# One attention and expert block on one core: the residual's x formed on VectorE from the projections' x

## The reference, cut to what matters

```python
def _layernorm(x, eps=1e-05):
    m = mean(x); v = var(x)
    return (x - m) / sqrt(v + eps)

def attn(x, ln1_w, Wq, Wk, Wv, rel_bias, scale, Wo, ln2_w, W1, W2):
    xn = rms_norm(x, ln1_w)                     # eps 1e-6
    q, k, v = heads(xn @ Wq), heads(xn @ Wk), heads(xn @ Wv)    # 16 heads of 8
    q, k = normalize(q), normalize(k)
    attn = (q @ k.T + bias) * scale, causal, softmax
    y = (attn @ v) @ Wo + x                     # <- the residual's x
    z = relu(rms_norm(y, ln2_w) @ W1) @ W2
    return z + y

x = L0_attn_x                                   # 8 images of 512 tokens of 128, float32
x = x + _layernorm(attn(_layernorm(x), ...))
x = x + _layernorm(moe(_layernorm(x), ...))     # top 2 of 8 experts
```

## Time and profile before

| | us |
|---|---|
| median of 3 runs | 609.92 |
| lowest and highest | 609.04, 613.66 |
| the profiled execution | 612.49 |
| span in the profile (first to last instruction) | 610.7 |
| mean granted TensorE clock | 0.955 of full speed |
| DMA | 55.85 MB, mean 91 GB/s |

### The profile page before, as it was taken

How to read it: one execution, slowest core, us unless ns; L and a number is a source line. 1 busy time by engine, 2 the same in 40 slices (tenths; PEclk the granted TensorE clock), 3 DMA queues, 4 the chain that set the end, 5 groups by cost and what they waited for, 6 DMA issues and landing times.

```text
span 610.7 us, 13818 instructions
## 1 busy us (share of the span) xinstructions
PE 532.2 (87%) x4568; PEld 386.2 (63%) x4569; DVE 382.8 (63%) x1083; ACT 396.6 (65%) x873; POOL 329.4 (54%) x337
## 2 busy tenths in 40 slices
PE   6876899989889899799899897899778979999992
PEld 5552355656466456465556564798678879999940
DVE  6627465783994974999947767363766434555344
ACT  3357898879779788878897786355353434554415
POOL 4012535536618888438877357176437754454426
PEclk9757799999999999999999999599999999999997
DMA  8755331223214323213734612022112332222074
GB/s 199 111 140 115 110 99 57 78 76 103 67 41 126 102 68 115 77 36 123 178 109 148 145 51 49 11 60 64 37 44 66 89 89 62 59 62 61 18 275 137
DMA packets 48285, 55.85 MB, mean 91 GB/s; under 512 B 7868, under 2 KB 42559, under 8 KB 46064
## 3 DMA queue, kind: packets, MB, share of 16 engines
q1 hardware_dynamic: 43872, 46.59, 28.3%
q0 software_dynamic: 4352, 8.47, 4.2%
HBM read 37.19 MB, written 18.36 MB: 91 GB/s over the span
## 4 chain that ended last, share of the span: by engine, by line
PE 49%; DVE 23%; POOL 11%; ACT 7%; issue 7%; DMA 3%; DVEq 1%; ACTq 0%; POOLq 0%; SPq 0%
PE SC L806 13%; PE OA L816 6%; PE OA L683 5%; PE M L757 4%; PE M L721 4%; POOL slots L1591 3%; DVE SS L1218 2%; POOL RZ L1577 2%; PE SC L665 2%; DVE arena L406 2%; DVE A L1477 2%; ACT arena L927 2%; DVE STP L1287 1%; PE SC L669 1%; PE M L649 1%
## 5 line engine op out<-in xcount | busy, mean ns | idle before, releaser
L927 ACT ACTIVATE arena<-SC 128x1024 f32<-128x1024 f32 x160 | 163.0, 1033 | 20.8 <-PE SC L670 12.3
L806 PE MATMUL SC<-arena 128*128 128x128 f32 (+1 forms) x864 | 110.8, 279 | 10.9 <-DVE arena L1385 10.9
L1597 POOL DMA_INDIRECT ytok<-YSA,XGA x72 | 74.8, 1038 | 80.4 <-ACT YSA L1030 71.5
L806 PEld LDWEIGHTS SC<-arena 128*128 128x128 f32 (+1 forms) x864 | 102.5, 186 | 14.0 <-DVE arena L1385 12.8
L683 PE MATMUL OA<-arena 128*32 128x256 f32 (+1 forms) x1536 | 91.4, 357 | 10.0 <-DVE arena L1251 6.1
L1591 POOL DMA_INDIRECT slots<-XBA,IDX x64 | 74.4, 1162 | 47.6 <-DVE IDX L1336 31.1
L1024 ACT ACTIVATE arena<-SC 128x256 f32<-128x256 f32 (+1 forms) x144 | 39.2, 324 | 78.2 <-PE SC L806 78.1
L1379 DVE TENSOR_TENSOR arena<-arena,SC 128x256 f32<-128x256 f32 (+1 forms) x144 | 44.2, 348 | 70.0 <-ACT arena L1024 70.0
L683 PEld LDWEIGHTS OA<-arena 128*32 128x32 f32 x1536 | 39.4, 110 | 49.6 <-issue 19.8
L406 POOL TENSOR_TENSOR arena<-arena 128x512 f32<-128x512 f32 x32 | 41.5, 1298 | 53.8 <-ACT arena L927 53.4
L816 PE MATMUL OA<-arena 128*128 (+1 forms) x432 | 60.2, 275 | 0.7 <-DVE arena L1379 0.7
(11 more groups left out here) (216 smaller groups left out, 1002.1 us busy)
## 6 DMA issues: line engine op xcount, KB each, us to landing
arena<-parts SPq DMA_DIRECT2D x90, 192.0 KB
parts<-arena SPq DMA_DIRECT2D x16, 384.0 KB, 2.5
XGA<-slots SPq DMA_DIRECT2D x72, 65.0 KB
arena<-ytok SPq DMA_DIRECT2D x8, 512.0 KB, 6.9
X<-in_L_attn_x SPq DMA_DIRECT2D x4, 512.0 KB, 5.3
arena<-toe SPq DMA_DIRECT2D x16, 128.0 KB, 5.9
out<-X SPq DMA_DIRECT2D x8, 256.0 KB, 2.3
arena<-parts SPq DMA_DIRECT2D x12, 96.0 KB
```

The costliest lines, as they stand in the source:

```text
L806: mm = pe.matmul(SC[0:n, r % 2, 512 * m + P * c:512 * m + P * (c + 1)], WSEL[r % 2][:, I * m + i0:I * m + i0 + n], XGT[r % 2], start=True, ...
L927: act.activation(EB[u], SC[:, n % 2, :], ACT.Exp).then_inc(exp_done, 1)
L1597: pool.indirect_dma_start(out=ytok_d.ap(), out_offset=bass.IndirectOffsetOnAxis(ap=XG[r][:, D + 1:D + 2].bitcast(I32), axis=0), in_=YS[r], ...
```

## The change

- XA, the semaphore xa_rdy and the function `xa` with its four activations per image go.
- At wo, DVE forms the sum from the projections' x: Y = XAR x RAT + M1, with one factor RAT per token, in four scalar_tensor_tensor of 128x128 in place of one addition of 128x512.
- XAR must live until then. It becomes XARS, three buffers, taken in turn; ACT waits for the transposes and the wo of the image three before.
- RAT is made in `x_roots` by two more DVE instructions, ahead of the one that signals st_rdy: residual's root times projections' root times the projections' variance.
- To make room, the scratch SCM of `slot_table` goes; the table uses one scratch in NW in place, so that its two reductions no longer stand back to back.

```diff
-ACT_AT = (dict(..., xar=-7, xa=1),
-    dict(..., h3=11, xa=0))
+ACT_AT = (dict(..., xar=-7),
+    dict(..., h3=11))
...
-        XA = sb("XA", [P, T, D])
+        XARS = [sb(f"XAR{r}", [P, T, D]) for r in range(2)] + [arena[:, 29184:29696].rearrange("p (t c) -> p t c", t=T)]
-        XAR = arena[:, WALL0 + 6656:WALL0 + 7168].rearrange("p (t c) -> p t c", t=T)
-        NWA = sb("NWA", [P, P])
-        NWB = sb("NWB", [P, P])
-        NWC = sb("NWC", [P, P])
+        RAT = sb("RAT", [P, NT])
+        NW = sb("NW", [P, 3 * P])
+        NWA, NWB, NWC = (NW[:, P * k:P * (k + 1)] for k in range(3))
-        SCM = sb("SCM", [P, 2, max(FIRST, EARLY - FIRST, STILES - EARLY), E])
+        PAST = NW[:, P:3 * P]
...
-                turn4(M0, XAR).then_inc(m0_full, 1)
+                turn4(M0, XARS[b % 3]).then_inc(m0_full, 1)
...
-                if b > 0:
-                    act.wait_ge(m0_full, USES0 * (b - 1) + 1)
-                norm(XAR, b, 1).then_inc(xar_rdy, 1)
-
-            def xa(b):
-
-                if b > 0:
-                    act.wait_ge(*drained(b, "wo"))
-                norm(XA, b, 0).then_inc(xa_rdy, 1)
+                if b >= 3:
+                    act.wait_ge(m0_full, USES0 * (b - 3) + 1)
+                    act.wait_ge(*drained(b - 2, "wo"))
+                for t in range(T):
+                    i = T * b + t
+                    ins = act.activation(XARS[b % 3][:, t, :], X[:, i, :], ACT.Identity, bias=NM0[:, 1, i:i + 1], scale=RSR[:, 1, i:i + 1])
+                ins.then_inc(xar_rdy, 1)
...
                 link(dve.scalar_tensor_tensor(y, u, 1.5, y, ALU.add, ALU.mult))
+                link(dve.tensor_tensor(RAT[:, i0:i1], y[:, 0, :], y[:, 1, :], ALU.mult))
+                dve.tensor_tensor(RAT[:, i0:i1], RAT[:, i0:i1], a[:, 1, :], ALU.mult)
...
                 elif k == "wo":
-                    dve.wait_ge(xa_rdy, b + 1)
-                    dve.tensor_tensor(Y[:, :, :].rearrange("p t d -> p (t d)"), M1[:, :],
-                                      XA[:, :, :].rearrange("p t d -> p (t d)"), ALU.add).then_inc(free1(body, k), 1)
+                    dve.wait_ge(xar_rdy, b + 1)
+                    for t in range(T):
+                        i = T * b + t
+                        last = dve.scalar_tensor_tensor(Y[:, t, :], XARS[b % 3][:, t, :], RAT[:, i:i + 1], M1[:, P * t:P * (t + 1)],
+                                                        ALU.mult, ALU.add)
+                    last.then_inc(free1(body, k), 1)
...
-                past, up = SCM[:, 0, 0:n], SCM[:, 1, 0:n]
+                past = PAST[:, 0:n * E].rearrange("p (n e) -> p n e", e=E)
                 link(dve.tensor_tensor(past, SIO[:, 0:n].unsqueeze(2).broadcast_to(sh),
                                        NTF[:, 1, :].unsqueeze(1).broadcast_to(sh), ALU.is_ge))
-                link(dve.tensor_tensor(up, past, NTF[:, 2, :].unsqueeze(1).broadcast_to(sh), ALU.mult))
                 row, exp = SRF[:, 0, s0:s0 + n], SRF[:, 1, s0:s0 + n]
-                dve.tensor_reduce(row, up, AX, ALU.add)
                 link(dve.tensor_reduce(exp, past, AX, ALU.add))
+                link(dve.tensor_tensor(past, past, NTF[:, 2, :].unsqueeze(1).broadcast_to(sh), ALU.mult))
+                link(dve.tensor_reduce(row, past, AX, ALU.add))
```

More of the change, by code:

```diff
@@ L45 @@
     dict(rx=0, logits=1, vsum=0, count=3, o0=3, o1=4, yt=5, wo=6, zt=7, h0=8, h1=9, h2=10, h3=11, ffn_a=12, ffn=12))
-ACT_AT = (dict(val=2, seed=1, xt=-5, qk0=-3, qk1=-2, out0=12, out1=1, rx=2, rexp=5, yt=4, ysq=10, zt=7, h0=9, h1=9, h2=10, h3=10, xb2=3, part0=4, half0=5, last0=7, part1=8, half1=9, last1=10, xar=-7, xa=1),
-    dict(out1=0, rx=0, xb2=1, rexp=3, yt=5, zt=7, ysq=9, h0=8, h1=9, h2=10, h3=11, xa=0))
+ACT_AT = (dict(val=2, seed=1, xt=-5, qk0=-3, qk1=-2, out0=12, out1=1, rx=2, rexp=5, yt=4, ysq=10, zt=7, h0=9, h1=9, h2=10, h3=10, xb2=3, part0=4, half0=5, last0=7, part1=8, half1=9, last1=10, xar=-7),
+    dict(out1=0, rx=0, xb2=1, rexp=3, yt=5, zt=7, ysq=9, h0=8, h1=9, h2=10, h3=11))
 DVE_AT = (dict(norm0=-2, norm1=1, norm2=1, lg=2, top2=3, vsum=0, o0=1, o1=1, wo=5, ffn=13, place=6, tab0=6, tab1=9, ln=16, xb=19),
@@ L197, in block_kernel @@
         W1R = OS[:, :, :].rearrange("p a b -> p (a b)")[:, 3 * D:3 * D + HID]
-        SCM = sb("SCM", [P, 2, max(FIRST, EARLY - FIRST, STILES - EARLY), E])
+        PAST = NW[:, P:3 * P]
+        assert E * max(FIRST, EARLY - FIRST, STILES - EARLY) <= 2 * P
         XGA = sb("XGA", [P, RING * ROW])
@@ L242, in block_kernel @@
         st_rdy = sem("st_rdy")
-        xa_rdy = sem("xa_rdy")
         dve_step = sem("dve_step")
@@ L967, in x_seeds, with xar @@
                 act.activation(RSR[:, :, n0:n1], RSR[:, :, n0:n1], ACT.Exp, scale=-0.5).then_inc(rseed_rdy, 1)
-            def norm(dst, b, r):
+            def xar(b):
+                act.wait_ge(st_rdy, min(b, 1) + 1)
+                if b >= 3:
+                    act.wait_ge(m0_full, USES0 * (b - 3) + 1)
+                    act.wait_ge(*drained(b - 2, "wo"))
                 for t in range(T):
                     i = T * b + t
-                    ins = act.activation(dst[:, t, :], X[:, i, :], ACT.Identity, bias=NM0[:, r, i:i + 1], scale=RSR[:, r, i:i + 1])
-                return ins
-            def xar(b):
-                act.wait_ge(st_rdy, min(b, 1) + 1)
-                if b > 0:
-                    act.wait_ge(m0_full, USES0 * (b - 1) + 1)
-                norm(XAR, b, 1).then_inc(xar_rdy, 1)
-            def xa(b):
-                if b > 0:
-                    act.wait_ge(*drained(b, "wo"))
-                norm(XA, b, 0).then_inc(xa_rdy, 1)
+                    ins = act.activation(XARS[b % 3][:, t, :], X[:, i, :], ACT.Identity, bias=NM0[:, 1, i:i + 1], scale=RSR[:, 1, i:i + 1])
+                ins.then_inc(xar_rdy, 1)
             def first_part(b, m):
@@ L1094, in _ @@
                             pre_copy(due(PRE[name], b, n), k)
-                    if 1 <= b <= NB:
-                        c = b - 1
-                        if n == at["xa"]:
-                            xa(c)
                     if b < NB and n == at["out0"]:
```

## The result

| | before | after |
|---|---|---|
| median, us (14 runs each) | 611.85 | 617.33 |
| lowest and highest, us | 608.97, 616.13 | 613.20, 619.97 |
| ratio of the times, 95% interval | | 1.0084 (1.0063 to 1.0106) |
| the profiled execution: time, span, us | 612.49, 610.7 | 617.38, 615.6 |
| mean granted clock | 0.955 | 0.947 |

The change costs 5.1 us by the ratio (0.84%; the medians lie 5.5 us apart), where +1.5 us was forecast and 615.0 was the upper end of the range. The kernel before, 609.92 us in the three runs that the forecast started from, is at 611.85 in fourteen. The shares of the page of after, answering to the earlier trace rows: ACT is busy 11 us less, as meant, and nothing else has shrunk.

What follows compares the result with a forecast made beforehand. No engine was taken as full (TensorE busy 87% of the span, most of the chain on PE). Terms 0.28 + 1.04 - 0.75 + 0.32 + 0.44 + 0.12 = +1.45 us took the median from 609.92 to 611.4 us, range 607.5 to 615.0.

Steps and rivals of the forecast that it cites:

- one place: Body 2: POOL's multiplication at 130.94 would still follow DVE's last scaling, by 0.14 us; another 0.1 us and POOL is first.
- POOL's scatters in body 3 are late by 0.44 us and no more: Body 3: indices for the scatters come 0.44 us later; a small gap on POOL takes 0.12 us, 0.32 us stay.
- the first two tables cost 0: Slot tables: the first two are made while others wait for POOL or ACT, so the new order costs 0.
- ACT's 0.25 us, bodies 2, 4, 6: Copy of OA starts at 127.44, not 127.69, after TensorE's product; 3 x 0.25 = 0.75 us won.
- Rival 1: Bodies 2, 4, 6: XA on the chain returns in full, 3 x 1.54 = 4.6 us won, 607.5 us; chance 0.12.
- hands the 0.25 us on: Bodies 2, 4, 6: TensorE, waiting for XBT before o1's transposes, passes on ACT's 0.25 us, DVE's YN being ready early enough.
- The addition: DVE at wo: 0.44 us longer per image; costs 4 x 0.26 us (bodies 1, 2, 4, 6), 0.32 (body 3), 0.44 (body 5).
- the term of 0.44 us: Body 5: longer addition delays the scatters' indices; POOL's chain has no gap up to the root, so 0.44 us stay.
- Start, table, bodies 7 and 8, buffers: RAT at the start +0.28 us; last table +0.12; bodies 7 and 8 hide the addition and win nothing; buffers cost 0.
- Rival 2: Bodies 2, 3, 5: POOL's multiplication gets SBUF first, DVE's scaling waits some 1.28 us; 3.25 us slower, 614.6; chance 0.2.
- price of 0.44 us in body 2: POOL-first case, body 2: YN at 134.52 instead of 133.24, TensorE wanting it at 134.23, priced at 0.44 us.
- 614.6 and 616.7: POOL-first times: 614.6 us in the short form; 616.7 if POOL's second multiplication also comes between; chance 0.2, 0.07 of it longer.

Runs made afterwards that it cites:

- e4: Changed kernel, with DVE's copy of VROW waiting until POOL has done both first-group multiplications in bodies 2, 4 and 6: ratio 1.0039.
- e5: Changed kernel, with four activations of 128x128 put back on ACT where XA's stood, in bodies 1 to 6: ratio 1.0066.
- e8: The changed kernel itself once more, no edit, against the kernel before: ratio 1.0077.
- e9: Changed kernel, VROW copy behind POOL's multiplications (bodies 2, 4, 6), second scatter behind POOL's second-group multiplications in body 3 only: ratio 1.0047.
- e14: Same kernel as e4, run once more: ratio 1.0072.
- e1: Changed kernel with one 128x512 addition at wo again, RAT left out and not formed (ACT's part alone): ratio 1.0012.
- e15: Same kernel as e1, run once more: ratio 1.0054.
- e2: Kernel before, with the addition at wo made in four scalar_tensor_tensor (XA times 1.0 plus M1): ratio 1.0039.
- e16: Same kernel as e2, run once more: ratio 1.0023.
- e6: Changed kernel with e4's wait, and the first pair's second scatter behind POOL's second-group multiplications in bodies 3, 5, 7: median 614.39 us, ratio 1.0044.
- e11: Kernel before, with POOL waiting between its two first-group multiplications for DVE's copy of VROW in bodies 4 and 6: ratio 1.0003.
- e3: Kernel before, with the two small DVE instructions that make RAT added at the start: ratio 1.0000.
- e7: Kernel before, with the first pair's second scatter moved behind POOL's second-group multiplications in bodies 3, 5 and 7: ratio 0.9999.

## Why the prediction was wrong

The forecast took the two engines' order at SBUF as fixed but for one place. Three steps of it failed: that 0.25 us are handed on in bodies 4 and 6, that POOL's scatters in body 3 are late by 0.44 us and no more, and that the first two tables cost 0.

- **ACT's 0.25 us, bodies 2, 4, 6**: right in size (0.19 us, TensorE's wait 0.83 for 1.02) and in its reason, that the copy of OA stands at TensorE's product anyway. Rival 1 is out. But "hands the 0.25 us on" is the step that failed: in bodies 4 and 6 what was handed on ended at DVE's copy of VROW coming ahead of POOL, 1.05 us lost in each for 0.19 won, and once a fall of the clock for some 1.6 us more.
- **The addition**: 0.44 us right (1.12 for 0.69). At zt it cost 0.14 us and not 0.26. In body 3 I let POOL's queue be 0.44 us late and no more; it crossed DVE's multiplication, and 0.9 us were lost, not 0.32.
- **Body 5**: the term of 0.44 us came as said, 0.43 to 0.46 us at 276 us in every trace with the four additions and the scatter in its place; on the slower chips it does not add to the 0.55 us that the kernel before loses there by itself. What the change adds is DVE's wait of 2.87 us, 1.4 us lost with it. It is in every trace that has both the four additions and the new order of the table, and no mend there (after, e4, e5, e8, e9, e14), and in none with only the table (e1, e15) or only the additions (e2, e16). Since e5 has it with ACT's time put back, it isn't XA's removal. The traces show how the two meet. From the start of body 5's table to DVE's L405 the new order takes 6.64 us and the old one 6.51, priced at 0 in the forecast. With it DVE's multiplications start 0.2 us ahead of POOL's second scatter and not 0.46, and the scatter takes 1.30 us and not 1.06. With the additions ACT's exp for POOL is over by the scatter's end (282.50 against 282.98 in after), and POOL's multiplications follow at once. Where both hold, POOL comes first; with the additions alone (e2) POOL follows at once too, and DVE comes first. With the table alone the exp is later, POOL waits 0.15 us more, and DVE comes first (timelines of POOL and DVE, e1):

```profile
281.85 1.30 POOL L1577 DMA_INDIRECT slots<-XBA,IDX  x1 [0.30 <-issue]
283.31 1.35 POOL L405 TENSOR_TENSOR arena<-arena 128x512 f32<-128x512 f32 x1 [0.15 <-ACT arena L926]
```
```profile
282.84 0.68 DVE L405 TENSOR_TENSOR arena<-arena 128x512 f32<-128x512 f32 x1
```

All traces agree with this, but the table and the additions without the rest were not tried, so it is argued and not shown.
- **Start, table, bodies 7 and 8, buffers**: +0.28 us is there at 10 us and drowned by the clock by 74 us; the last table's chain is 0.06 us longer, not 0.12 (offsets +4.35 at 456 us, +4.41 at 465); the rest 0, as said.
- **Rival 2** had the mechanism, and in e6 and in body 5 also the form. Its place was wrong: DVE's scalings take 1.43 us as before in all bodies. Its price of 0.44 us in body 2 doesn't follow from its own numbers either (134.52 less 134.23 is 0.29); that its 614.6 and 616.7 lie nearer the measured time than the forecast does is luck. I looked for one place where POOL passes DVE and priced it; the change shifts three chains by unlike amounts, and every pair of a DVE and a POOL instruction in them was a candidate.

Added up, against 0.55 us for the kernel before: ACT's part 2.1 us (3.4 with the clock's fall), the addition's 1.5, DVE's wait in body 5 where all is together 1.4, together 5.0 to 6.3; the changed kernel's two traces lose 5.4 and 5.9 (5.9 and 6.5 if the 0.55 us belong to the slower chips alone). The ratios of the parts (0.33% and 0.31% in the mean of two each) fall 0.1 to 0.2% short of the whole. The wait in body 5 would fill that, but it is less than the uncertainty of some 0.3% of each run.

The Trainium skill, page "SBUF — State Buffer", section "SBUF: two separate sides", gives a rule of who starts first and holds the port pair for the whole instruction. The trace agrees that a wait is for whole instructions, but here the loser waited for several: in body 4 POOL's, from 216.57, for DVE's until 218.92, and in body 5 DVE's, from 282.67, for the rest of a scatter and two multiplications of POOL's until 284.97.

What stays open is who comes first when both stand waiting. In body 4 DVE's copy starts 0.20 us before POOL's first multiplication ends, in the kernel before (218.41; 217.31 + 1.30) and in the changed one (216.42; 215.34 + 1.28) alike, yet where nothing forces the order POOL came first in all seven traces with ACT's four activations and DVE in all four without. It hangs on ACT's time; by what, no trace shows. In body 5 too the recorded starts do not tell: DVE's multiplication starts 0.33 us ahead of POOL's both where it comes first (before) and where it comes second (after). Nor is it shown why the same wait of TensorE is followed by a fall of the clock in some executions and not in others.

## What to carry to other kernels

When a change shifts one of two engines that hold each other up, as DVE and POOL do here, list every pair of their instructions that lie within a few tenths of a microsecond before and after, not the one place that looks closest: each cost 0.9 to 2.2 us of waiting here and turned round with a shift of 0.1 to 0.4 us. A semaphore wait that fixes the order where it matters (e4) keeps such a place from turning, here with no cost that its traces show. Take the mend's gain from the times as well as from the trace: the traces of e4, e5 and e14 lose some 3 us less than the changed kernel's, and 7 to 12 executions of each did not show it. One trace is one draw: a second trace of the unchanged kernel, had it been at hand, would have shown which of its rows are chance.

## What was not expected of the hardware

- A POOL multiplication of 0.74 us stood for 2.2 us more because DVE issued four instructions in a row; a DVE instruction of 8 elements a partition took 2.05 us and not 0.15, behind POOL.
- A wait of TensorE of 1.0 us in a stretch at full clock was followed by 2 to 4 us at or near 0.50 in body 4 twice (after, e8) and in body 6 once (e15), and by none in e1 and e11 for the same wait or 0.75 us. Behind a wait of 1.6 us in body 5 the clock fell in e4, e5 and e14 and not in after, e8 and e9. Between 80 and 380 us it fell in none of the two traces of the kernel before and in none of e2, e3, e7 and e16.
- With identical instructions up to there, executions differ by up to 3 us at 74 us through the time at which the clock rises.
